# Second feed-forward: match keys loaded through DRAM, and two down-product units placed behind the last expert pair

## The reference, cut to what matters

```python
x = L0_attn_a_x                                   # (8, 512, 512) f32
x = x + scan(layernorm(x))                        # selective scan
x = x + ffn(layernorm(x))
x = x + attention(layernorm(x))
x = x + ffn(layernorm(x))                         # the second feed-forward: the change is here

def ffn(hidden_states):                           # E=64 experts, top K=6, H=512, I=352, capacity 64
    scores = softmax(x @ gate_w.T); topk_w, topk_i = top_k(scores, 6)
    # each expert takes at most 64 of the tokens that chose it, in order of token
    y = einsum('eci,eih->ech', silu(buf @ w_gate) * (buf @ w_up), w_down)   # per expert
    out = sum over a token's kept slots of y[expert, slot] * weight
    shared = silu(x @ sw_gate) * (x @ sw_up) @ sw_down                      # width 704
    return out + shared
```

## Time and profile before

| | |
|---|---|
| median of 3 runs | 2992.32 us (2991.42 to 2997.06) |
| the profiled execution | 3004.71 us |
| its span in the profile | 3002.9 us |
| PE, DVE, ACT, POOL busy | 2714.2, 1786.8, 1294.0, 1507.0 us |
| DMA | 566.13 MB |

### The profile page before, as it was taken

One profiled execution on the slowest core, in us unless ns is written; L12 is line 12 of the kernel. 1 busy time (PEld: TensorE's weight loads), 2 busy tenths in 40 slices (PEclk: granted clock), 3 DMA queues, 4 the chain that ended last, 5 costly groups with the idle time before them and its releaser, 6 DMA issues.

```text
span 3002.9 us, 37450 instructions
## 1 busy us (share of the span) xinstructions
PE 2714.2 (90%) x13484; PEld 1431.3 (48%) x13484; DVE 1786.8 (60%) x3809; ACT 1294.0 (43%) x2693; POOL 1507.0 (50%) x928
## 2 busy tenths in 40 slices
PE   4668988998988879999969999999899999999998
PEld 2454555555545534443335555555544444444443
DVE  5999999999999852222246666665524444222222
ACT  4657576675857411111127676766712220111111
POOL 5998999999998801222136555554400001121211
PEclk7779999999999889999989999999999999999999
DMA  5454545545554379999930000001135324899997
GB/s 190 152 191 155 191 162 164 192 159 184 172 166 163 125 307 367 396 392 393 362 109 1 29 29 29 29 29 67 39 100 198 116 74 170 305 383 336 362 337 215
DMA packets 168234, 566.13 MB, mean 189 GB/s; under 512 B 22832, under 2 KB 24752, under 8 KB 167536
## 3 DMA queue, kind: packets, MB, share of 16 engines
q1 hardware_dynamic: 149904, 521.65, 47.0%
q0 software_dynamic: 17088, 40.90, 5.9%
q10 hardware_dynamic: 1056, 1.18, 0.1%
HBM read 487.89 MB, written 75.79 MB: 188 GB/s over the span
## 4 chain that ended last, share of the span: by engine, by line
PE 53%; DVE 3%; ACT 2%; POOL 2%; DMA 2%; issue 1%; POOLq 0%; SPq 0%; DVEq 0%; ACTq 0%
PE bank L1174 10%; PE bank L1077 5%; PE bank L1098 5%; PE bank L1200 5%; PE bank L1112 5%; PE bank L1225 5%; PE bank L1282 4%; PE bank L1259 3%; PE bank L1247 2%; PE bank L1271 2%; POOL arena L2004 2%; DMA scratch_y<-arena 2%; PE bank L1157 1%; PE bank L1213 1%; ACT arena L1824 1%
## 5 line engine op out<-in xcount | busy, mean ns | idle before, releaser
L1906 POOL TENSOR_TENSOR arena<-arena 128x1024 f32<-128x1024 f32 x256 | 606.7, 2373 | 14.3 <-PE bank L1027 9.6
L1753 ACT ACTIVATE bank<-arena 128x512 f32<-128x512 f32 x512 | 345.7, 688 | 327.5 <-DVE arena L1376 177.4
L2004 POOL TENSOR_TENSOR arena<-arena 128x2048 f32<-128x2048 f32 (+3 forms) x128 | 296.7, 2321 | 276.0 <-DVE arena L1611 276.0
L1027 PE MATMUL bank<-arena 128*128 128x128 f32 x2048 | 294.1, 297 | 121.3 <-POOL arena L1914 120.5
L1824 ACT ACTIVATE arena<-arena 128x256 f32<-128x256 f32 (+3 forms) x512 | 287.2, 565 | 149.1 <-DVE arena L1602 125.4
L1027 PEld LDWEIGHTS bank<-arena 128*128 128x128 f32 x2048 | 254.1, 153 | 201.1 <-POOL arena L1914 149.0
L1376 DVE TENSOR_TENSOR_SCAN bank<-bank,arena 128x512 f32<-128x512 f32 x272 | 326.6, 1206 | 3.9 <-ACT bank L1753 2.7
L1914 POOL TENSOR_TENSOR arena<-arena 128x512 f32<-128x512 f32 x240 | 311.0, 1296 | 24.6 <-DVE arena L1376 24.3
L1174 PE MATMUL bank<-arena 128*64 128x352 f32 x2048 | 323.2, 469 | 0.0
L1376 DVE TENSOR_TENSOR_SCAN arena<-bank,arena 128x512 f32<-128x512 f32 x240 | 291.2, 1213 | 18.6 <-ACT bank L1753 9.7
L1077 PE MATMUL bank<-arena 128*128 128x512 f32 x640 | 292.5, 600 | 6.0 <-ACT arena L1715 3.1
(11 more groups left out here) (149 smaller groups left out, 4160.1 us busy)
## 6 DMA issues: line engine op xcount, KB each, us to landing
arena<-scratch_bc SPq DMA_DIRECT2D x128, 1024.0 KB, 5.4
arena<-in_w_out SPq DMA_DIRECT2D x128, 768.0 KB, 15.4
arena<-in_w_gate SPq DMA_DIRECT2D x128, 704.0 KB, 10.8
arena<-in_w_up SPq DMA_DIRECT2D x128, 704.0 KB, 13.1
scratch_x<-arena SPq DMA_DIRECT2D x16, 1024.0 KB, 4.8
scratch_xn<-arena SPq DMA_DIRECT2D x15, 1024.0 KB, 4.2
arena<-scratch_x SPq DMA_DIRECT2D x44, 256.0 KB, 6.1
arena<-scratch_x SPq DMA_DIRECT2D x8, 1024.0 KB, 7.5
```

What stands on the lines that cost most here:

```text
L1027: i = nc.tensor.matmul(y[:, t * P:(t + 1) * P], w[:, n, t * P:(t + 1) * P], p.ident, is_transpose=True, start=False, stop=g == GROUPS - 1 ...
L1753: nc.scalar.activation(bank[p.da_bank(k, n)][:, :], block_of(p.dt, b, c), ACT.Exp, scale=p.alog[:, c, state:state + 1]).then_inc(*p.decaye ...
L1906: nc.gpsimd.tensor_tensor(out=p.hb[k % HB], in0=over(block_of(p.dtx, b, c), 1, NG), in1=p.bc[k // 2 % NBC][:, 0], op=ALU.mult).then_inc(*p ...
L2004: nc.gpsimd.tensor_tensor(out=own, in0=own, in1=over(p.rden[:, k % 2, :], 2, width), op=ALU.mult).then_inc(*p.divided.up(k))
```

## The change

Two things, both for m = 1 alone (`HELD = (0, 2)`).

The keys: SP stores `tok`'s even rows (the 64 slots of each pair's first expert) to DRAM after `merge` (`keys_out`, 8 KB), and loads all 32 x 64 of them back into each of the 128 partitions with one broadcast DMA (`keys_in`, 1 MB) before the loads of experts 3 and 4. `match` reads them from SBUF; the transpose in `expert_up` and the two waits on its account go.

The held units: the last two down units (quad 7, tiles 0 and 1, tiles 2 and 3) aren't spread over the rounds any more. Their products follow the last `combine` on PE, then their copies on DVE, then their two sums on POOL. The two sums have a semaphore each in place of a slot in the order of adds: each waits for the feed-forward's last scatter and not for the other.

```diff
@@ front_plan
     plan += [("merge", m)] + units.spend(2)
-    plan += [("lists", m), ("turnover", m)]
-    plan += [("gather", m, p) for p in range(RING_X[m])] + units.spend(3)
+    plan += [("keys_out", m), ("lists", m), ("turnover", m)]
+    plan += [("gather", m, p) for p in range(RING_X[m])] + units.spend(3) + [("keys_in", m)]
     plan += [i for e in range(RING_W[m] - 2, RING_W[m]) for i in (("w_up", m, e), ("w_down", m, e))]
+def held_back(m, q, t):
+    return q == BATCH - 1 and t >= QT - HELD[m] * ABREAST[m]
@@ expert_plan
-    left = units.left()
+    last = units.units[:HELD[m]]
+    last.reverse()
+    held = sum(map(units.size, last))
+    tiles = [i for unit in last for i in unit if i[0] == "sd"]
+    left = units.left() - held
...
-            plan += units.spend(units.left() - left * (NPAIR - 1 - p) // NPAIR)
+            plan += units.spend(units.left() - held - left * (NPAIR - 1 - p) // NPAIR)
+        elif ABREAST[m] == 1:
+            plan += tiles[:1]
...
-    assert not units.units
+    units.units.clear()
+    plan += tiles[ABREAST[m] == 1:]
+    plan += [i for unit in last for i in unit if i[0] == "so"]
@@ expert_up (PE)
             PE.wait_ge(p.hidden, m, k - 1)
+        if k > 0 and m == 0:
             PE.wait_ge(p.matched, m, k - 1, 0)
-        nc.tensor.transpose(bank[2][:, INTER:INTER + CAP], f["key"][0:CAP, k:k + 1].to_broadcast([CAP, P]),
-                            p.ident[0:CAP, 0:CAP])
+        if m == 0:
+            nc.tensor.transpose(...)
@@ match (DVE)
-        V.wait_ge(p.up_made, m, k)
+        if m == 0:
+            V.wait_ge(p.up_made, m, k)
+        else:
+            V.wait_ge(p.keys_in, m)
...
-        nc.vector.tensor_scalar(same, bank[2][:, INTER:INTER + CAP], f["key"][:, k:k + 1], None,
+        same, keys = f["same"][k % 2], f["keys"][:, k, :] if m else bank[2][:, INTER:INTER + CAP]
+        nc.vector.tensor_scalar(same, keys, f["key"][:, k:k + 1], None,
@@ shared_sum (POOL)
+        held = held_back(m, q, t)
...
-        wait_order(key, m)
+        if held:
+            G.wait_ge(p.added, last_add(m))
+        else:
+            wait_order(key, m)
+        signal = p.held_added[m, q, t].up(m, q, t) if held else p.added.up(key)
@@ SP
+    def keys_out(m):
+        SP.wait_ge(p.slotted, m, 1)
+        nc.sync.dma_start(d["keys"], p.ff[m]["tok"][0:E:2, :]).then_inc(*p.keys_out.up(m))
+
+    def keys_in(m):
+        SP.wait_ge(p.keys_out, m)
+        nc.sync.dma_start(p.ff[m]["keys"].rearrange("p k s -> p (k s)"),
+                          d["keys"].rearrange("k s -> (k s)").partition_broadcast(P)).then_inc(*p.keys_in.up(m))
```

More of the change, by code:

```diff
@@ L94 @@
 GIVEN_LATE = (False, True)
+HELD = (0, 2)
 BARE = (2, 4, 6)
@@ L667, in memory @@
         self.expert_memory(sb, 1)
+        self.ff[1]["keys"] = sb.cut([NPAIR, CAP])
     def norm_work(self, sb):
@@ L863, in semaphores @@
         adds = [("so", *i[1:]) if i[0] == "so" else ("give", *i[1:]) for i in self.plan
-                if i[0] == "give" or i[0] == "so" and i[2] >= DIRECT[i[1]] and i[3] == last_abreast(i[1], i[3])]
+                if i[0] == "give" or i[0] == "so" and i[2] >= DIRECT[i[1]] and i[3] == last_abreast(i[1], i[3])
+                and not held_back(*i[1:])]
         self.add_order = {k: i for i, k in enumerate(adds)}
@@ L867, in semaphores @@
         self.added = Signal(self, "rows_added", [(k,) for k in adds], 16)
+        self.held_added = {i[1:]: Signal(self, "held_added_%d_%d" % (i[1], i[3]), [i[1:]], 16) for i in self.plan
+                           if i[0] == "so" and held_back(*i[1:]) and i[3] == last_abreast(i[1], i[3])}
         self.route_set = sig("route_set", "route_w", parts=range(2))
@@ L890, in semaphores @@
         self.listed = sig("listed", "lists")
+        self.keys_out, self.keys_in = sig("keys_out", "keys_out", by=16), sig("keys_in", "keys_in", by=16)
         self.matched = sig("matched", "match", parts=range(3))
@@ L1166, in expert_up @@
             PE.wait_ge(p.hidden, m, k - 1)
+        if k > 0 and m == 0:
             PE.wait_ge(p.matched, m, k - 1, 0)
-        nc.tensor.transpose(bank[2][:, INTER:INTER + CAP], f["key"][0:CAP, k:k + 1].to_broadcast([CAP, P]),
-                            p.ident[0:CAP, 0:CAP])
+        if m == 0:
+            nc.tensor.transpose(bank[2][:, INTER:INTER + CAP], f["key"][0:CAP, k:k + 1].to_broadcast([CAP, P]),
+                                p.ident[0:CAP, 0:CAP])
         for w, made in ((0, p.gate_made), (1, p.up_made)):
@@ L1429, in wait_so_free @@
                 V.wait_ge(p.so_stored[i % OUT[m]], m, q, t)
+            elif held_back(m, q, last_abreast(m, t)):
+                V.wait_ge(p.held_added[m, q, last_abreast(m, t)], m, q, last_abreast(m, t))
             else:
@@ L1550, in match @@
         V.wait_ge(p.ring_with("lists", m).taken_by["dve"], "lists", m)
-        V.wait_ge(p.up_made, m, k)
+        if m == 0:
+            V.wait_ge(p.up_made, m, k)
+        else:
+            V.wait_ge(p.keys_in, m)
         if k >= 2:
             V.wait_ge(ring.made, "combine", m, k - 2)
-        same = f["same"][k % 2]
-        nc.vector.tensor_scalar(same, bank[2][:, INTER:INTER + CAP], f["key"][:, k:k + 1], None,
+        same, keys = f["same"][k % 2], f["keys"][:, k, :] if m else bank[2][:, INTER:INTER + CAP]
+        nc.vector.tensor_scalar(same, keys, f["key"][:, k:k + 1], None,
                                 ALU.is_equal).then_inc(*p.matched.up(m, k, 0))
@@ L1933, in route_w, with last_add @@
         G.wait_ge(p.route_set, m, 1)
+    def last_add(m):
+        return [k for k in p.adds if k[1] == m][-1]
     def wait_order(key, m):
@@ L1946, in shared_sum @@
         key, n = ("so", m, q, t), ABREAST[m]
-        if key not in p.add_order:
+        if t != last_abreast(m, t) or q < DIRECT[m]:
             return
+        held = held_back(m, q, t)
         ring, i = p.ring_with("sd", m, q, t), q * QT + t
@@ L1952, in shared_sum @@
         G.wait_ge(p.y_copied, m, q)
-        wait_order(key, m)
+        if held:
[3 more added lines that the diff above has]
+        signal = p.held_added[m, q, t].up(m, q, t) if held else p.added.up(key)
         rows = p.d["out" if m else "y"][(i + 1 - n) * P:(i + 1) * P, :]
         nc.gpsimd.dma_start(rows.rearrange("(t p) h -> p t h", t=n), p.ff[m]["so"][:, s + 1 - n:s + 1, :],
-                            accum_op=ALU.add).then_inc(*p.added.up(key))
+                            accum_op=ALU.add).then_inc(*signal)
     def turnover(m):
@@ L2036, in sums @@
         SP.wait_ge(p.added, [k for k in p.adds if k[1] == m][-1])
+        for key, signal in p.held_added.items():
+            if key[0] == m:
+                SP.wait_ge(signal, *key)
     def x_in(b):
@@ L2206, in sync_engine @@
             "bc_out": bc_out, "bc_in": bc_in, "x1": x1, "xn_out": xn_out, "fetch": fetch, "so": so, "xt_in": xt_in,
-            "pads": pads, "w_up": w_up, "w_down": w_down, "route1": route1, "turnover": turnover, "xa_in": xa_in,
+            "pads": pads, "w_up": w_up, "w_down": w_down, "route1": route1, "turnover": turnover,
+            "keys_out": keys_out, "keys_in": keys_in, "xa_in": xa_in,
             "attn_w": attn_w, "x3": x3}
@@ L2270, in lay_out @@
     }
-SCRATCH = {"bc": (BATCH, 2 * NSTATE, SEQ), "x1": (T, H), "x3": (T, H),
+SCRATCH = {"bc": (BATCH, 2 * NSTATE, SEQ), "keys": (NPAIR, CAP), "x1": (T, H), "x3": (T, H),
            "y": (T + PAIR, H), "xn": (T + CAP, ROW)}
```

## The result

The changed kernel takes 2990.24 us in the median of 21 runs, the one before 2997.06 on the same chips; the ratio is 0.9975, 95% interval 0.9968 to 0.9983. That is 7.5 us less (5.1 to 9.6); 7.85 were forecast. The forecast time of 2984.5 stood on the median of 3 runs of the kernel before, 2992.32; with 21 runs that median is 2997.06, so it is the difference that is compared and not the time. Single executions of one kernel lie up to 14 us apart, so what follows is read from stretches inside one trace and not from the ends of two: the profiled execution of after has a span 15.1 us shorter, of which 7.3 are there by 2484 us, before the first instruction that the change adds (the store of the keys, at 2497.31).

A forecast was written before the change was run, and what follows sets the result against it. PE's full stream was taken to bound the expert stage, then the tail. Transposes (5.9) and held units (19.38) take 25.3 us off, the tail adds 17.45: -7.85 us, median 2984.5, range 2980.5 to 2990 (own range 2982.5 to 2987).

The forecast's parts named there:

- The transposes, 5.9 us: Second feed-forward's expert rounds: dropping 32 key transposes from PE saves 5.9 us (bounds 1.9 and 8.3).
- The load of the keys, nothing: Before the expert stage: the 1 MB broadcast load is charged nothing; without cover for the first gather, up to 2 us.
- The held units, 19.38 off and 17.45 on: Two down units leave the rounds, 9.69 us each; their products, copies and sums after the last combine add 17.45.
- The sums' semaphores buy nothing: Kernel's end: the two held sums no longer waiting for each other gains nothing; the second has nothing before it.
- The DMA stands it: Expert stage: about 150 MB in 427 us, 351 GB/s, holds; the trace shows 381 for 60 us without PE waiting.
- The room of 1.8 us: Two adjacent bare rounds, mid-stage: loads due in 13.5 us land in 5.8 to 11.7, so 1.8 to spare.
- Rival 3: Weights late in the two bare stretches, 2 us at each, 4 lost: 2988.5 us; chance 0.08.
- Rival 4: DMA bounds the whole expert stage at 334 GB/s: 22 us lost, ending slower at 3006.5; chance 0.07.
- Rival 1: Transposes in the expert rounds cost their whole busy time, 32 x 0.27 = 8.6 us: 2981.8; chance 0.13.
- rival 2: Transposes cost next to nothing in every round, 32 x 0.06 = 1.9 us: 2988.5; chance 0.06.
- Rival 5: First gather 2 us late and the last sum landing like a loaded one, 4 lost: 2988.5; chance 0.06.
- the last step, from a span to a median: Profiled execution forecast at 2996.9 us; the earlier kernel's 12.4 us gap between profiled and median runs gives 2984.5.

## Why the prediction was right

- *What bounds it: PE's stream, then the tail.* PE is busy throughout in all versions but the one with a quad held, and every time taken off its stream came off the whole.
- *The transposes, 5.9 us.* Alone they bring 5.8. The steps were read rightly: a bare round is 9.20 us (9.21 forecast), behind a sixth unit 0.30 are saved, behind a gate/up unit 0.20; behind a down unit it is 0.05 in half of the rounds and 0.10 in the others, where 0.1 was taken. The argument by a neighbour, how soon a product of the same shape follows the flip elsewhere, did it; the busy time of 0.27 would have given 8.6. That busy time was also called an outer bound for every round, which the 0.30 behind a sixth unit passes.
- *The load of the keys, nothing.* It lands in 6.0 us (bounds 4.8 to 11.1), and the start of the first round is not late: PE's wait of 1.39 us for DVE is what it was.
- *The held units, 19.38 off and 17.45 on.* Alone they bring 2.0 in all. Counted from the last up products, the second L1138 group starts at +32.05 (+32.04 forecast), POOL issues the second sum at +34.8 as forecast, it lands in 5.8, and the end is at +42.43 (+42.5).
- *The sums' semaphores buy nothing.* This is shown by chaining them.
- *The DMA stands it.* This is shown from both sides: there is no wait at 356 GB/s with two bare rounds together, and 4.6 us are lost at 382 with three together and bare rounds closer to each other. The room of 1.8 us was reckoned too small, since it set the landing of both experts' loads (11.7) against the time in which the first is due; by the packets it is 6.6 at the least. Rival 3 had a mechanism that exists, weights late behind bare rounds, but it takes more of them than the change makes. Rival 4, the DMA as the bound of the whole stage, was seen in no run. The 358 GB/s that the Trainium skill states ("DMA: Bandwidth & Descriptors", "Where 436 GB/s comes from") is not what binds here: the DMA moved 386 GB/s for 60 us in the changed kernel, and 382 over 385 us with a quad held.
- *Rival 1 and rival 2* are out by the stretch of the keys alone, 446.24, where they wanted 443.6 and above 450. *Rival 5* is out by the start of the first round and by the tail, neither of which is late.

What was near luck is the last step, from a span to a median: the two profiled executions, before and after, differ by twice the effect. The forecast difference held since it was a sum of steps inside one trace. The agreement to 0.35 us (7.5 and 7.85) is finer than the runs can tell, as their interval is 5.1 to 9.6.

## What to carry to other kernels

When one engine's stream is full, price an instruction by the step from its neighbour's start to the next one's, with and without it, and look in another place of the same trace for a turn that lacks it. Its busy time is not the price: here it was 0.27 us, and the price went from 0.05 to 0.30 with the neighbours. Work that doesn't depend on the last results can be put behind them so that their slow way out lies beside it, but the gain is only the difference of the two tails (2 us here for 19 us moved), and it ends where that work was covering loads. Where the effect is smaller than the scatter of executions, compare stretches inside the traces.

## What the runs showed of the hardware

- A transpose of 64 rows between one of 128 rows and products with 64 columns of weights cost 0.20 us, a second one behind it 0.06, and one of 128 rows and twice the columns in its place 0.11. Behind products of 64 rows, the one of 128 rows cost 0.20 more than the one of 64 (1.31 against 1.11).
- A PE wait of 2.27 us cost more than itself: in the 3 us behind it the granted clock was 0.50, the lower of the two levels (1.2 of 2.4 GHz), and the 32 up products took 6.39 us in place of 4.95. Behind the waits of 1.39 us at the start of the stage and 0.56 us at its end they took 4.95, no longer than elsewhere.
- With weight loads, gathers and scatters side by side, one core's DMA moved 386 GB/s over 60 us and 382 over 385 us.
